# Moving the upper half of a new GRU state from VectorE to ScalarE, one step later

## The reference, cut to what matters

```
h = x
for l in range(5):
    m = h @ weight[l]
    agg = A^T m
    r, z = sigmoid(gi_r + gh_r), sigmoid(gi_z + gh_z)      # gi = agg @ w_ih.T + b_ih, gh = h @ w_hh.T + b_hh
    n = tanh(gi_n + r * gh_n)
    h = (1 - z) * n + z * h
```

## Time and profile before

| | |
|---|---|
| median of 3 runs | 774.82 us (773.11 to 776.09) |
| the profiled execution | 774.86 us, of which 773.1 us is the span of its instructions |
| granted TensorE clock, mean | 0.989 |
| PE busy | 703.1 us (91%) |
| DVE busy | 600.1 us (78%) |
| ACT busy | 521.4 us (67%) |
| POOL busy | 298.9 us (39%) |

### The profile page before, as it was taken

How to read it: one execution, slowest core, us unless ns; L and a number is a source line. 1 busy time by engine, 2 the same in 40 slices (tenths; PEclk the granted TensorE clock), 3 DMA queues, 4 the chain that set the end, 5 groups by cost and what they waited for, 6 DMA issues and landing times.

```text
span 773.1 us, 12576 instructions
## 1 busy us (share of the span) xinstructions
PE 703.1 (91%) x4198; PEld 591.3 (76%) x4198; DVE 600.1 (78%) x1461; ACT 521.4 (67%) x1083; POOL 298.9 (39%) x423
## 2 busy tenths in 40 slices
PE   3899799989999988989999989989999988989897
PEld 2678588778888767878788767878878867868665
DVE  4698997888978967888977976788986787876343
ACT  5566677578777757767877867667777657657544
POOL 4212424563334343463344332574333232542420
PEclk9999999999999999999999999999999999999999
DMA  6520011100000020400000020210000000110001
GB/s 154 136 59 1 2 45 20 49 2 4 5 4 1 1 58 12 126 28 3 6 3 1 1 58 1 69 42 4 7 3 1 1 0 1 55 55 7 7 1 55
DMA packets 47623, 21.08 MB, mean 27 GB/s; under 512 B 9032, under 2 KB 47560, under 8 KB 47560
## 3 DMA queue, kind: packets, MB, share of 16 engines
q1 hardware_dynamic: 47560, 20.29, 9.8%
HBM read 15.27 MB, written 4.19 MB: 25 GB/s over the span
## 4 chain that ended last, share of the span: by engine, by line
PE 42%; DVE 30%; ACT 12%; POOL 9%; issue 5%; DMA 1%; DVEq 0%; SPq 0%; POOLq 0%; ACTq 0%
PE bank L405 7%; PE bank L407 7%; PE bank L406 7%; PE bank L400 5%; DVE zd L1327 4%; DVE hd L1339 4%; DVE h L1331 4%; POOL rstd L938 3%; DVE bank L1353 3%; DVE rh L1350 3%; ACT bank L910 2%; ACT xn L713 2%; PE bank L613 2%; DVE h_hi L1334 2%; ACT g_hi L893 2%
## 5 line engine op out<-in xcount | busy, mean ns | idle before, releaser
L954 POOL TENSOR_TENSOR h_lo<-h,h_hi 128x512 fp32r<-128x512 f32 x64 | 81.8, 1279 | 334.2 <-DVE h_hi L1334 334.2
L405 PE MATMUL bank<-h_hi,whh_hi 128*128 128x512 f32 x240 | 107.8, 449 | 13.4 <-DVE rh L1350 12.6
L1350 DVE SCALAR_TENSOR_TENSOR rh<-bank,rh 128x512 f32<-128x512 f32 x80 | 54.9, 687 | 66.9 <-ACT bank L904 66.8
L405 PE MATMUL bank<-g_hi,wc_hi 128*128 128x512 f32 x240 | 103.6, 432 | 0.7 <-DVE h L1331 0.3
L407 PE MATMUL bank<-h_lo,whh_hi 128*128 128x512 f32 x240 | 96.8, 403 | 0.0
L406 PE MATMUL bank<-h_hi,whh_lo 128*128 128x512 f32 x240 | 96.6, 403 | 0.0
L406 PE MATMUL bank<-g_hi,wc_lo 128*128 128x512 f32 x240 | 94.8, 395 | 0.0
L407 PE MATMUL bank<-g_lo,wc_hi 128*128 128x512 f32 x240 | 94.7, 395 | 0.0
L400 PEld LDWEIGHTS bank<-edge,hn 128*128 128x128 f32 x640 | 84.5, 193 | 10.3 <-DVE edge L1053 3.1
L713 ACT ACTIVATE xn<-x_res,shift,rstd 128x128 f32<-128x128 f32 x128 | 55.8, 486 | 50.2 <-POOL shift L940 50.0
L400 PE MATMUL bank<-edge,hn 128*128 128x128 f32 x640 | 85.3, 276 | 2.9 <-DVE edge L1053 2.9
(11 more groups left out here) (169 smaller groups left out, 1631.6 us busy)
## 6 DMA issues: line engine op xcount, KB each, us to landing
x_in<-in_x SPq DMA_DIRECT2D x8, 512.0 KB, 5.5
adj_in<-in_adj SPq DMA_DIRECT2D x8, 512.0 KB, 4.9
x_res<-in_x SPq DMA_DIRECT2D x16, 256.0 KB, 2.8
out_x<-x_res SPq DMA_DIRECT2D x16, 256.0 KB, 2.3
xz<-x_res SPq DMA_DIRECT2D x16, 50.0 KB
w_sb<-in_L_gnn_W SPq DMA_DIRECT2D x1, 640.0 KB, 5.6
w_sb<-in_L_gnn_W SPq DMA_DIRECT2D x5, 128.0 KB, 5.6
rows<-in_adj SPq DMA_DIRECT2D x32, 0.6 KB
```

The costliest lines, as they stand in the source:

```text
L405: nc.tensor.matmul(dst[:], w_hi, m_hi, start=start, stop=False)
L954: nc.gpsimd.tensor_tensor(h_lo[q][:], h[q][:], h_hi[q][:].bitcast(f32), ALU.subtract).then_inc(sem["h_lo_new"], 1)
L1350: nc.vector.scalar_tensor_tensor(rh[:], R_BANK[:], 1.0, rh[:], ALU.add, ALU.mult).then_inc(sem["rh_ready"], 1)
```

## The change

ACT makes `h_hi` of step n - 1 in step n, ahead of the tanh of r and behind the even slot's work. DVE's copy, with its wait, is taken out. POOL's low_half(n - 1) goes to the start of its step n, ahead of the even slot's work; it was behind the even slot's work of step n - 1, so it now stands behind the odd slot of step n - 1 also.

```diff
@@ ScalarE
+            def split_new(n):
+                act.wait_ge(sem["h_new"], n + 1)
+                nc.scalar.activation(h_hi[n % QUADS][:], h[n % QUADS][:], ACT.Copy).then_inc(sem["h_hi_new"], 1)
...
                 beside(2 * n)
+                if n and (n - 1) % STEPS < SPLITS:
+                    split_new(n - 1)
                 act.wait_ge(sem["gates_r"], n + 1)
@@ GpSimd
             for n in range(ALL + TAIL_STEPS):
+                if n and n <= ALL and (n - 1) % STEPS < SPLITS:
+                    low_half(n - 1)
                 beside(2 * n)
-                if n < ALL and n % STEPS < SPLITS:
-                    low_half(n)
                 beside(2 * n + 1)
@@ VectorE
                 nc.vector.scalar_tensor_tensor(h[q][:], zd[:], 0.5, I_BANK[:], ALU.mult, ALU.add).then_inc(sem["h_new"], 1)
-                if layer < LAYERS - 1:
-                    dve.wait_ge(sem["h_new"], n + 1)
-                    nc.vector.tensor_copy(h_hi[q][:], h[q][:]).then_inc(sem["h_hi_new"], 1)
```

## The result

The changed kernel takes 764.42 us (median of 4 runs, 763.7 to 765.15) against 774.83 us before (4 runs, 773.11 to 776.09): a ratio of 0.9868, 95% interval 0.9849 to 0.9886, or 10.4 us less. The forecast was 767.5 us in a range of 757 to 778. The direction and the range held; the gain is 3.2 us larger than forecast, and the interval (8.8 to 11.7 us) does not reach down to the 7.2 us that the sum gave.

What follows compares the result with a forecast made beforehand. No engine bounds the kernel throughout; the chain passes through all, PE holding 42%, DVE 30%. First round -2.8, rounds 1 and 2 -1.0 each, round 3 -2.4: -7.2 us against 774.86, forecast 767.5 us, range 757 to 778.

Steps and rivals of the forecast that it cites:

- DVE's copies gone: DVE's line loses 64 copies of 427 ns, claimed to save 0.34 to 0.43 us each on that line.
- `h_lo` out of the norm's way: Steps 12 and 13 of later rounds: power no longer waits behind low_half; 1.37 us each, 2.7 a round, copy included.
- five `blocks` products: Products that waited from 268.1 for `h_lo`; with step 31's `h_lo` run behind them in step 32, 0.66 us saved a round.
- ACT's copy on the chain: Steps 2, 11, 13 and 14 of each later round: copy delays the tanh of r, 4 x 0.57 = 2.3 us lost.
- stops at the port: Moved `h_lo` stops DVE: `mix` in steps 21, 24 (1.12, 1.18 us), `zd` in 27 to 29; net 3.7 us a round.
- ten places: Rounds 1 to 3, steps 0-3, 5-7, 9-11: DVE freed, eight times 0.34, twice 0.43, 3.6 us saved a round.
- Steps 14 and 15: Same form as steps 12 and 13, but where PE runs back to back (296 to 326 us): claimed to give nothing.
- The first round: Steps 4 to 10, DVE-bound: copies gone once 0.3, four times 0.43, 2.0 us; with step 16's 0.8, 2.8 us saved.
- Step 16's `zd`: Took 1.51 us beside POOL's add_identity, which no longer waits for `h_lo`; claimed 0.8 us saved, once.
- No loss at the port: Rival: `mix` gets in ahead of `h_lo` in steps 21 and 24 of each round; 760.8 us, chance 0.22.
- Swallowed by PE: Rival: another PE wait leaves about 0.6 of the 3.6 us a round, losses stay; 776.7 us, chance 0.16.
- The tanh of r passes its delay on: Rival: in PE's loops 22 more steps pass on 0.57 us each to `rh`, 12.5 us; 780 us, chance 0.12.

Runs made afterwards that it cites:

- no copy at all: Kernel before with DVE's copy taken out and none put in, low_half waiting for the state itself at its old place; 754.33 us, ratio 0.9728.
- POOL's order alone: Kernel before with only POOL's low_half(n - 1) moved to the start of step n, DVE keeping its copy; 769.84 us, ratio 0.9947.
- earlier copy: Kernel after with ACT's copy ahead of the even slot's work in steps 1, 2, 13 to 16 of later rounds; 759.96 us, ratio 0.9795.
- `h_lo` cut short: Kernel after with POOL's low_half cut to 4 of its 512 columns; 753.23 us, ratio 0.9735.
- the short copy on ACT: Kernel after with ACT's copy cut to 4 of its 512 columns, order and waits kept; 761.05 us, ratio 0.9838.

## Why the prediction was right, and where its size was off

The mechanism was right: a relief on DVE and in the norm's path, paid in part by ACT's copy on the chain and by stops at the port that POOL and DVE share. The sizes for each of the rounds 1 and 2, with what measures them (the terms are not quite independent of each other, so the sum of the measured ones is a check and no proof). The prediction had put DVE's share of steps 27 to 29, 0.34 us each, into the price of the stops; here it stands with the copies, as the experiments measure it.

| term of the sum | put at, us | measured, us | from |
|---|---|---|---|
| DVE's copies gone (3.6; 0.43 each in steps 32, 33; 0.34 each in 27 to 29) | -5.5 | -5.4 and -6.5 | no copy at all |
| `h_lo` out of the norm's way, beyond the copy | -1.8 | -2.4 | POOL's order alone: -1.4, after a stop of 0.96 |
| five `blocks` products | -0.7 | -0.65 | step 31: -1.12 after, -0.47 with no copy |
| ACT's copy on the chain | +2.3 | +2.9 | earlier copy, 5 x 0.52; the chain, 2 x 0.52 in steps 28 and 30; less 0.8 of step 36 |
| stops at the port: `mix` 2.3, `zd` 2.4 | +4.7 | +3.7 | `h_lo` cut short: `mix` 2.06, `zd` 0.74, `deg_some` 0.94 |
| sum | -1.0 | -1.8 and -2.9 | after: -2.3, and -2.4 without the clock's 1.55 |

**The step that failed** is the first: "eight times 0.34, twice 0.43 = 3.6 us", too small in its price and short of places. The price was read between the start of the copy and the start of what follows; it had to be read from the start of the state, because the copy's wait for the state also takes away the overlap of two neighbours. Where DVE is on the path throughout a copy was worth 0.46. The ten places did not all give that: in the kernel without a copy steps 20, 21, 26, 27 and 29 to 31 are shorter by 0.41 to 0.47 us, 23 and 25 by 0.15 and 0.19, and 22 is 0.18 longer. Together they gave 3.3, 4.2 and 3.9 us in the rounds 1 to 3. The rest came from steps that the sum left out: 8 and 15 of a round with 0.41 to 0.47 us each, 4 and 14 with 0.15 to 0.18.

In rounds 1 and 2 a second fault hides this: the shares of steps 27 and 29 stand among the ten places and were taken off the stops once more, 0.7 us counted twice. That the first row then comes out right in round 1 is luck. In round 3, which has no stops of `zd`, nothing hides it: -4.5 was put, -5.8 measured, and that is more than half of what the round gave beyond its forecast.

**ACT's copy** was put on the chain in four places a round, those ahead of the tanh of r in steps 2, 11, 13 and 14 (the lengths of steps 21, 30, 32 and 33 in round 1). There it stands, at 0.52 and not 0.57. But it stands there in three more: ahead of steps 9, 15 and 16, which were put at nothing. Step 36 gives part of that back.

**The stops of `zd`** were the second wrong size, in the other direction: 0, 0.37 and 0.37 us in steps 27 to 29, against 0.55, 0.84 and 1.02. `h_lo` started 3.4 us ahead of `zd` and not 3.0 (236.65 against 239.65 in the prediction's working), so POOL's row of work was over earlier. The stop of `deg_some`, which no term had, filled half of that gap. `mix` cost 0.99 and 1.07 where 1.12 and 1.18 were forecast; the first of these needs no ACT, since POOL's order alone makes it.

**Steps 14 and 15** were put at nothing. With POOL's order alone steps 34 and 35 give 0.17 and 1.03 and step 36 takes 0.71 back: half a microsecond a round, which is what the second row of the table has in excess. Most of it is a stop at the port in the kernel before, which no list had. First step 35 before, then with POOL's order alone:

```profile
305.50 1.27 POOL L954 TENSOR_TENSOR h_lo<-h,h_hi 128x512 fp32r<-128x512 f32 x1 [6.87 <-DVE h_hi L1334]
305.62 1.69 DVE L1265 SCALAR_TENSOR_TENSOR x_res<-scaled,x_res 128x512 f32<-128x512 f32 x1
```
```profile
303.98 0.66 DVE L1265 SCALAR_TENSOR_TENSOR x_res<-scaled,x_res 128x512 f32<-128x512 f32 x1
```

`x_res` loses its stop of 1.03 us once `h_lo` has left its place behind the copy; without a copy but in POOL's old order it still takes 1.69. Steps 32 and 33 gave 0.96 each, as put (1.37 less the copy's 0.43).

**The first round** gave -1.7 and not -2.8; 0.66 of the difference is the stop of `ones_r`, and the copies gave less than the 2.0 us put: the kernel without one gains 1.55 in the whole round, step 16 included. Step 16's `zd`, put at 0.8, gave 0.92 with the copy's share and 0.56 by POOL's order alone. The last round gave 2.2 us more than put: 1.3 by the copies, 0.5 by POOL's order, and the rest is not assigned to a place.

**The rivals.** "No loss at the port" falls: `mix` does not get in ahead. "Swallowed by PE" falls with the kernel without a copy: 5.4 to 6.5 us of a round remain, and steps 26 to 33 keep 0.44 to 0.48 each. PE's idle time ahead of its second convolution in step 27, 0.54 us in the earlier trace rows, is down to 0.10 (in step 28, behind a stopped `zd`, it grew from 0.33 to 0.67), and `sup` stands 0.61 us behind `h`:

```profile
228.42 0.69 DVE L1337 SCALAR_TENSOR_TENSOR h<-zd,bank 128x512 f32<-128x512 f32 x1
229.03 0.28 DVE L1234 COPY sup<-bank 100x128 f32<-100x128 f32 x1
```

"The tanh of r passes its delay on" falls as a whole: the kernel is faster, and the short copy on ACT gets back 3.4 us, where the rival's places alone would have given 9. In part it holds: the chain passes the copy in step 28, which the sum did not have, and in steps 26 and 27 the short copy gets back 0.14 and 0.19 us of its 0.43, while the short `h_lo` gets back nothing there. The rule on elementwise work that the prediction cited from the Trainium skill ("ScalarE: Activation LUTs", section "Rules for kernel authors") has the order of the engines' prices right here (626 ns against 427) and the direction of this change wrong: what decides is which of the two stands in the chain.

## What to carry to other kernels

Price an instruction that is to leave an engine from the start of its predecessor to the start of its successor, with and without it: a wait for the predecessor's end costs the overlap too. When an operation moves to another engine, the one that consumes it moves with it: look where that one then starts, and which instruction of VectorE stands within its length, those with two inputs in SBUF first, those from SBUF to SBUF too. Then choose the place step by step; here three places for one copy, by what each step had to spare, were worth 8.6 us on top of the change's 10.4.

## What the runs showed of the hardware beyond that

- A one-input instruction of 128x9 elements was stopped by POOL for about as long as a two-input one of 128x512: `deg_some` 1.16 us for 0.17.
- Of a POOL and a DVE instruction, the one that started first held the other up in these cases: in step 24 above POOL was 1 ns ahead and `mix` took 1.83 us, in step 21 of the kernel after POOL was 0.13 us ahead (`h_lo` at 170.79, `mix` at 170.92) and `mix` took 1.68. In step 23 of the kernel after `mix` was 0.12 us ahead (190.69 against 190.81): it took its 0.69 us, and `h_lo` 1.71.
- The lower level of the clock came mostly in single stretches of 3.4 us, in or behind a wait of PE (one of 1.75 us ahead of the stretch at 382.5), at other steps in other kernels, and not behind every such wait. Inside the steps 44, 45, 64 and 65 one costs 1.3 to 1.9 us, which is as much as some of the edits above; two kernels that differ by less than that should be compared step by step and not by their medians.
